# A decoder layer on one core: batch loops written out, attention without a gap between batches, buffers by parity in place of copies

## The chip, the cores and the metric

One core of a Trainium2 chip runs the whole program. The time is the device time of one execution in microseconds (us), median of several runs. Engines are named PE (matmul), PEld (its weight loads), DVE, ACT, POOL and SP; SP here only issues DMAs, and a DMA is waited for through a semaphore.

## The reference, cut to what matters

Eight batches of 512 positions with 256 features, float32. Three blocks, each added to its input:

```
x = x + mamba2_block(layernorm(x))         # in_proj, causal conv of 4 taps, silu, selective scan
x = x + attention(layernorm(x), ctx, ctx)  # 16 heads of 16; scores/4 + adj, masked keys at -inf
x = x + experts(layernorm(x))              # position picks 1 of 8 matrices 256x256 (+ bias)
```

Inside `mamba2_block` the input is normalised once more, then `z`, `xBC` (768 channels) and `dt` (8 heads) are projected, `xBC` goes through the convolution and silu, `dt` through softplus; the scan `h = h*exp(dt*A) + dt*x*B`, `y = h.C + D*x` runs over the 512 positions; `y*silu(z)` is RMS-normalised and projected back to 256. Attention takes its queries from the normalised result and keys and values from `ctx`, adds `adj` (512x512) and the mask to the scores, and projects with `Wo`. The experts are chosen by position alone, the same for all batches.

## The kernel before, in words

**Sizes.** 512 positions are C = 4 chunks of P = 128. The scan is done in chunks by matmuls: per chunk a decay matrix (`seg`, on `L`), the Gram matrix and transposes (`gx`), the gate projection (`z`), products with the carried state (`inter`), within the chunk (`intra`) and for the next state (`state`), then gate, RMS norm, transpose (`o`), output projection (`x1`) and the query's layer norm (`xq`).

**Attention units.** One unit is one head and one tile of 128 queries: UNITS = 64 in a batch, in G = 4 groups of UG = 16 units (four heads). For unit u, PE makes scores in `ps[u%2]` (`score`, the call through `mm`, L474), DVE adds the bias `am` and takes the row maximum into `T` and `nmx` (`take_max`, L1153), ACT takes the exponential in place (L806), and three units later (LAG) PE transposes the row block into `pt` (`turn`, L609), and ACT (L820) or, for five units of each sixteen, DVE (L1166) moves it to `PT`. After a group PE multiplies with the values (`pv`, L622, into `po`), ACT copies the sums to `OTs` (L824), PE turns them back (L629) and DVE divides (L1171, L1174). Q and K were written to DRAM in a high and a low part (`out_parts`) and are loaded two heads at a time into `q_st`, `k_st` (`stage`), eight DMAs each time; stage 0 of a batch is loaded before its attention, stage 1 at its start.

**Order of the work.** Every engine runs its own instruction list. The lists are built slot by slot from one table: slot u holds the attention's unit u of batch a and the stages of other batches that the tables `MAIN`, `CHUNK` (at slots 7, 17, 27, 37) and `NEXT` put there. One body has SLOTS = 64 + 15 slots. It works on three batches at a time: attention of a, everything from K to the queries of b = a+1, and the head (layer norms, `dt`, `bc` projections, convolution, `cum`) of a+2. In slots 64 to 78 no unit begins: the last units drain, the output projection runs over `ps` and `pt` (`project_turn` L636, `project`), and the rest of the next head is done. The bodies of the first two calls without attention, of a = 0 and of a = 6 and 7 are written out; those between are a hardware loop (`eng.Fori`), SP's with one batch fewer. Semaphore targets inside the loop are computed in registers (`alone`).

**Buffers.** Values, score bias and the residual rows are made in `vm`, `am_m`, `x1` and copied by DMA to `va`, `am`, `x1a` for the attention that follows. The smaller matmuls share three PSUM banks `pm` in a fixed rotation, `M_TILES`: 56 tiles a batch; a tile may be written when the tile three before it has been read (`m_full`, `m_read`).

**Beginning and end.** After the head of batch 0, `between` runs on all engines: a 1-of-8 routing of positions to experts, mostly on DVE with a few small matmuls. After the last attention come the experts: gather by position, layer norm, matmuls, scatter.

Of the kernel before, what the change touches and what calls it, by code (L numbers as in the profile page):

```python
# [42 lines left out]
PROJ = UNITS + LAG + 3  # L43

EVAC_DVE = (1, 5, 7, 11, 15)
DRAIN = 15
SLOTS = UNITS + DRAIN
NT = 8
PD = 32
# [15 lines left out]
HEAD = ("ln1", "ln2", "lnT", "dt1", "dt2", "bc", "conv", "cum")  # L65
# [3 lines left out]
MAIN = {  # L69
    ("k", 0): (0, {}), ("k", 1): (1, {}), ("ksplit",): (2, {"sp": 1}), ("v", 0): (2, {"dve": 1}), ("v", 1): (3, {"dve": 2, "sp": 1}),  # L70
    ("silu", 4): (1, {"dve": 1}), ("silu", 5): (2, {"dve": 1}), ("silu", 0): (3, {"dve": 2}), ("silu", 1): (4, {"dve": 1}),
    ("silu", 2): (5, {"dve": 1}), ("silu", 3): (6, {"dve": 1}), ("am", 0): (10, {}), ("am", 1): (12, {}), ("am", 2): (13, {}), ("am", 3): (16, {}),
    ("q1",): (50, {}), ("q2", 0): (51, {}), ("q2", 1): (52, {}), ("qsplit",): (53, {"sp": 1}),
}

CHUNK_AT = (7, 17, 27, 37)
CHUNK = {
    ("dmask",): (0, {}), ("seg", 0): (1, {}), ("seg", 1): (1, {}), ("gx",): (2, {"dve": 1, "pool": 1}), ("z",): (3, {"act": 1, "dve": 2}),
    ("w",): (4, {}), ("inter",): (5, {"dve": 1}), ("sdec",): (6, {}), ("intra",): (6, {"dve": 1}), ("state",): (7, {"dve": 2}), ("gate",): (8, {}),
    ("gate2",): (9, {}), ("o",): (9, {}), ("x1",): (10, {"dve": 1, "pool": 1}), ("xq",): (12, {}),  # L80
}

NEXT = {
# [4 lines left out]
}  # L88


def schedule():


    when = {e: [[] for _ in range(SLOTS)] for e in ("sp", "pe", "act", "dve", "pool")}

    def put(stage, slot, shift):
        for e in when:
            when[e][slot + shift.get(e, 0)].append(stage)
# [1317 lines left out]
```

## Time and profile before

| | |
|---|---|
| time, median of 3 runs (us) | 1533.87 (1533.64 to 1536.82) |
| span of the profiled execution (us) | 1529.4 |
| its own whole time | not listed beside the span; the median is 4.5 us above the span |
| instructions | 24283 |
| PE, DVE, ACT, POOL busy (us) | 1228.2, 1021.7, 776.9, 576.2 |
| mean granted PE clock | 0.932 of full speed |
| DMA | 117.20 MB, of which 1.62 MB instructions |

The span runs from the first to the last instruction of one execution. Busy time is the union of an engine's recorded instructions. Matmuls are pipelined and their ends are modelled, so PE's busy time is an upper figure. A time stands at the start of each row of a timeline; what is in square brackets behind a row is the engine's idle time before it and what ended it, "issue" meaning that nothing in the profile did.

### The profile page before, as it was taken

To read this page: it belongs to the slowest core of one execution; us is meant where nothing else is said; L and a number is where in the kernel's file an instruction comes from. 1 tells how busy PE (TensorE), PEld (TensorE's weight loads), DVE (VectorE), ACT (ScalarE), POOL (GpSimd) and SP (SyncE) were. 2 spreads that over 40 slices of the span, in tenths; PEclk is the share of its full clock that TensorE was granted. 3 is DMA by queue.
4 is the path that set the end of the run, shared out by engine and by line. 5 is a ranking of instruction groups with operands and counts; after the bars stand their busy time and mean duration, and the time that the engine had idled before them with its cause. 6 is when DMAs were issued, how large, how long until landed. Compare 5 with 4: busy or idle time off the path is not lost.

```text
span 1529.4 us, 24283 instructions
## 1 busy us (share of the span) xinstructions
PE 1228.2 (80%) x7020; PEld 787.0 (51%) x7020; DVE 1021.7 (67%) x2572; ACT 776.9 (51%) x1380; POOL 576.2 (38%) x533
## 2 busy tenths in 40 slices
PE   1577778878898789888888799878997889777488
PEld 1344445645565456555665456535654566454344
DVE  1655476876776577766687567758668667476376
ACT  0122156654566366645565356636564566577333
POOL 1725364335331723153333533172324532010165
PEclk9779789999999999988999899989999899999889
DMA  5020412134202331133212421234102321331321
GB/s 154 9 69 1 159 61 56 42 97 139 56 29 70 126 97 29 44 111 110 56 42 93 138 57 32 65 113 109 34 29 99 108 56 42 111 90 42 139 88 65
DMA packets 67713, 117.20 MB, mean 77 GB/s; under 512 B 16160, under 2 KB 26656, under 8 KB 65280
## 3 DMA queue, kind: packets, MB, share of 16 engines
q1 hardware_dynamic: 57808, 95.58, 19.5%
q0 software_dynamic: 6240, 17.57, 5.0%
q10 hardware_dynamic: 3536, 2.43, 0.6%
q8 instruction: 69, 1.13, 0.3%
q14 instruction: 60, 0.49, 0.1%
HBM read 71.49 MB, written 27.26 MB: 65 GB/s over the span
## 4 chain that ended last, share of the span: by engine, by line
PE 48%; DVE 25%; issue 13%; ACT 9%; POOL 3%; DMA 1%; SPq 1%; DVEq 1%; ACTq 0%; POOLq 0%
PE pm L474 21%; PE po L622 8%; DVE T L1153 6%; PE pt L609 5%; PE ps L474 4%; ACT PT L820 3%; ACT T L806 3%; PE ps L712 2%; PE pt L474 2%; DVE PT L1166 2%; DVE xc L1137 1%; DVE L L1061 1%; DVE xc L1142 1%; PE po L629 1%; DVE kp L1125 1%
## 5 line engine op out<-in xcount | busy, mean ns | idle before, releaser
L806 ACT ACTIVATE T<-T,nmx 128x512 f32<-128x512 f32 x512 | 369.2, 723 | 335.5 <-DVE nmx L1153 333.0
L1153 DVE CUSTOM_DVE_ANT_0 T<-ps,am 128x512 f32<-128x512 f32 x512 | 350.0, 687 | 272.3 <-PE ps L474 248.5
L609 PE MATMUL pt<-ident,T 128*128 128x128 f32 x2048 | 323.5, 283 | 63.2 <-ACT PT L820 62.6
L609 PEld LDWEIGHTS pt<-ident,T 128*128 128x128 f32 x2048 | 251.4, 145 | 175.3 <-ACT PT L820 59.6
L474 PE MATMUL ps<-k_st,q_st 128*128 128x512 f32 x512 | 306.6, 599 | 24.3 <-DVE nmx L1153 12.9
L820 ACT COPY PT<-pt 128x512 f32<-128x512 f32 x352 | 200.0, 571 | 55.1 <-PE po L622 54.4
L622 PE MATMUL po<-PT,va 128*32 128x512 f32 x1024 | 126.5, 638 | 29.7 <-DVE PT L1166 22.7
L474 PEld LDWEIGHTS ps<-k_st,q_st 128*128 128x128 f32 x512 | 101.9, 199 | 81.8 <-issue 59.2
L1244 POOL TENSOR_TENSOR xc<-xc,ygT 128x512 f32<-128x512 f32 x96 | 130.3, 1357 | 10.3
L1166 DVE COPY PT<-pt 128x512 f32<-128x512 f32 x160 | 109.8, 686 | 9.4 <-PE pt L609 9.0
L474 PE MATMUL pm<-xnT,wxbc 128*128 128x512 f32 x192 | 94.4, 625 | 0.0
L1295 POOL TENSOR_TENSOR rr<-se,nhalf 128x1 f32<-128x1 f32 x32 | 21.8, 681 | 191.8 <-DVE se L1096 191.8
L1273 POOL TENSOR_TENSOR xdt<-xt,dt 128x512 f32<-128x512 f32 x32 | 34.4, 1074 | 151.3 <-ACT xt L778 151.3
L474 PE MATMUL pm<-wout,ygT 128*128 128x256 f32 x256 | 66.8, 406 | 26.9 <-ACT ygT L786 26.7
L622 PEld LDWEIGHTS po<-PT,va 128*32 128x32 f32 x1024 | 32.6, 116 | 101.0 <-issue 73.4
L1241 POOL TENSOR_SCALAR ygT<-pre,cw 128x512 f32<-128x512 f32 x96 | 74.1, 772 | 9.8 <-POOL xc L1244 7.4
L474 PE MATMUL pm<-xdt,L 128*128 128x64 f32 x512 | 63.3, 277 | 12.1 <-issue 11.1
L474 PEld LDWEIGHTS pm<-xdt,L 128*128 128x128 f32 x512 | 60.2, 193 | 20.4 <-issue 20.4
L474 PEld LDWEIGHTS pm<-wout,ygT 128*128 128x128 f32 x256 | 47.9, 197 | 40.2 <-ACT ygT L786 21.2
L474 PE MATMUL pm<-L,stril 128*128 128x512 f32 x128 | 66.3, 644 | 0.8 <-POOL L L1265 0.8
L1265 POOL TENSOR_TENSOR L<-triu,dA 128x1024 f32<-128x1024 f32 x32 | 66.0, 2063 | 0.0
L1236 POOL TENSOR_SCALAR xc<-pre,cw,cb 128x512 f32<-128x512 f32 x32 | 28.6, 895 | 94.4 <-ACT pre L746 94.4
(208 smaller groups left out, 1995.3 us busy)
## 6 DMA issues: line engine op xcount, KB each, us to landing
qk_d<-kp SPq DMA_DIRECT2D x64, 256.0 KB, 2.4
q_st<-qk_d SPq DMA_DIRECT2D x256, 64.0 KB, 2.2
k_st<-qk_d SPq DMA_DIRECT2D x256, 64.0 KB, 2.2
am_m<-in_mask SPq DMA_DIRECT2D x8, 1024.0 KB, 7.4
am_m<-in_adj POOLq DMA_DIRECT2D x8, 1024.0 KB, 9.8
am<-am_m SPq DMA_DIRECT2D x16, 512.0 KB, 3.5
va<-vm SPq DMA_DIRECT2D x8, 1024.0 KB, 4.6
x_in<-in_x SPq DMA_DIRECT2D x8, 512.0 KB, 4.1
```

What stands on the lines that cost most here:

```text
L474: return pe.matmul(out, lhsT, rhs, start=first, stop=last)
L609: ins = pe.transpose(pt[u % 2][:, kt * P:(kt + 1) * P], T[:, u % RING, kt * P:(kt + 1) * P], ident[:, :])
L622: ins = pe.matmul(po[VW * hh:VW * (hh + 1), :], va[:, kt, g * HG + hh, :], PT[:, hh, kt, :], start=(kt == 0), stop=(kt == C - 1), tile_pos ...
L712: ins = pe.matmul(ps[w % 2][SEG * j:SEG * (j + 1), h * E:(h + 1) * E], t_f[:, w % 2, (h * KE + kt) * P + SEG * j:(h * KE + kt) * P + SEG * ...
L806: act.activation(T[:, u % RING, :], T[:, u % RING, :], ACT.Exp, bias=nmx[:, u % RING:u % RING + 1], scale=-1.0).then_inc(sems["probs"], 1)
L820: act.copy(PT[:, hh, :, qt * P:(qt + 1) * P], pt[v % 2][:, :].rearrange("p (k i) -> p k i", i=P)).then_inc(sems["evac_act"], 1)
L1153: dve.tensor_tensor_reduce(T[:, u % RING, :], ps[u % 2][:, :], am[:, qt, :], -1.0, 3e38, ALU.add, ALU.min, nmx[:, u % RING:u % RING + 1]). ...
L1166: dve.tensor_copy(PT[:, hh, :, qt * P:(qt + 1) * P], pt[v % 2][:, :].rearrange("p (k i) -> p k i", i=P)).then_inc(sems["evac_dve"], 1)
L1241: pool.tensor_scalar(tap[:, :, :].rearrange("p k i -> p (k i)"), src[:, j:j + S], cw[:, mt, j:j + 1], 0.0, ALU.mult, ALU.add).then_inc(sem ...
L1244: pool.tensor_tensor(xc[:, mt, :], xc[:, mt, :], tap[:, :, :].rearrange("p k i -> p (k i)"), ALU.add).then_inc(sems["conv_pool"], 1)
L1265: pool.tensor_tensor(dmask[:, :, :], triu[:, :].rearrange("p (o i) -> p o i", o=1).broadcast_to([P, NH, P]), dA[:, c, :].rearrange("p (h o ...
L1273: pool.tensor_tensor(xdt[:, :, :], xt[:, :, :], dt[:, c, :].rearrange("p (h o) -> p h o", o=1).broadcast_to([P, NH, HD]), ALU.mult).then_i ...
```

## The change: what it does

1. **Loops written out.** `batches`, `Fori`, `alone` and the register targets go. Each engine has one list over SLOTS = LEAD + 8 x 64 + 16 slots, LEAD = 92. `M_TILES` becomes a table of (tile, batch) over the whole program.
2. **No gap.** Unit u of batch a is at slot LEAD + 64 a + u; the next batch's unit 0 follows unit 63 directly, and the three units, the `pv`, and the projection that were in the drain now stand between the next batch's units.
3. **Stage table anew.** `STAGES`, `CHUNK`, `TAIL` give for each stage and each engine an own place, in slots (with fractions for the order within one) counted from the same batch's unit 0. `ln2` is split: `xn` at -82, `xr` (`ln2r`) at -65.75. The routing (`between`) is after slot -65 of batch 0.
4. **Buffers by parity.** `vas`, `ams`, `x1s` are pairs, used by batch parity; the copies `vm` to `va`, `am_m` to `am`, `x1` to `x1a` go. The mask for a batch is loaded two batches' buffers apart. A further memset prepares the second `va`. `xq` lies in `xr`, `xqT` in `th`.
5. **Output projection** as tiles `ot` (transposes) and `op` (matmuls) in the rotation of `pm`: 64 tiles a batch. It is at 69.5 to 77.5, in units 5 to 13 of the next attention.
6. **Waits** that the body's order gave are now written, mostly on tiles of batch b - 1; `more_consts` is waited for in single stages of batch 0.

```diff
-PROJ = UNITS + LAG + 3
-DRAIN = 15
-SLOTS = UNITS + DRAIN
+DVE_SETUP = 10
+SETUP_AT = -65
...
-MAIN = {
-    ("k", 0): (0, {}), ("k", 1): (1, {}), ("ksplit",): (2, {"sp": 1}), ("v", 0): (2, {"dve": 1}), ("v", 1): (3, {"dve": 2, "sp": 1}),
...
-    ("q1",): (50, {}), ("q2", 0): (51, {}), ("q2", 1): (52, {}), ("qsplit",): (53, {"sp": 1}),
+STAGES = {
+    ("ln1",): {"dve": -89.75, "pool": -89.5}, ("ln2",): {"dve": -82}, ("ln2r",): {"sp": -63.75, "dve": -65.75, "pool": -68},
+    ("lnT",): {"pe": -80.5, "act": -80.75}, ("dt1",): {"pe": -78.75, "act": -76.75, "dve": -78.5}, ("bc", 4): {"pe": -79, "act": -79.75},
+    ("conv", 4): {"pool": -71.75}, ("bc", 5): {"pe": -73.5, "act": -72.25}, ("conv", 5): {"dve": -70.25}, ("bc", 0): {"pe": -72, "act": -70.25},
+    ("conv", 0): {"pool": -70.25}, ("bc", 1): {"pe": -70.75, "act": -70.25}, ("conv", 1): {"dve": -66.5}, ("bc", 2): {"pe": -65.25, "act": -66},
+    ("conv", 2): {"pool": -59.5}, ("bc", 3): {"pe": -64.25, "act": -65}, ("conv", 3): {"pool": -55.5}, ("dt2", 0): {"dve": -76},
...
+    ("silu", 2): {"act": -59.5, "dve": -54.75}, ("silu", 3): {"act": -57, "dve": -54.75}, ("q1",): {"pe": -13.75, "act": -14},
+    ("q2", 0): {"pe": -12.75, "act": -11.5}, ("q2", 1): {"pe": -11.5, "act": -11.25}, ("qsplit",): {"sp": -9.5, "dve": -9.5}, ("first",): {"sp": -7.25},
 }
-CHUNK_AT = (7, 17, 27, 37)
+CHUNK_AT = (-56, -46, -36, -27)
 CHUNK = {
-    ("dmask",): (0, {}), ("seg", 0): (1, {}), ("seg", 1): (1, {}), ("gx",): (2, {"dve": 1, "pool": 1}), ("z",): (3, {"act": 1, "dve": 2}),
...
+    ("dmask",): {"pool": 1.5}, ("seg", 0): {"pe": 2.25, "act": 2}, ("seg", 1): {"pe": 1.5, "act": 1.5},
+    ("gx",): {"pe": 2.5, "act": 2.75, "dve": 3.25, "pool": 7.25}, ("z",): {"pe": 4.25, "act": 4.25, "dve": 5.25}, ("w",): {"dve": 5},
+    ("inter",): {"pe": 5.5, "dve": 6.5}, ("sdec",): {"pool": 8.75}, ("intra",): {"pe": 6.75, "dve": 7}, ("state",): {"pe": 7.5, "dve": 8.75},
+    ("gate",): {"act": 7, "dve": 7.25}, ("gate2",): {"dve": 8.25, "pool": 10.25}, ("o",): {"pe": 8.75, "act": 8.25},
+    ("x1",): {"pe": 10, "dve": 11, "pool": 11.75}, ("xq",): {"dve": 12.5, "pool": 19.25},
 }
-NEXT = {
-    ("ln1",): (47, {}), ("ln2",): (54, {}), ("lnT",): (55, {"sp": 1}), ("dt1",): (58, {"dve": 1, "act": 2}), ("bc", 4): (60, {}),
-    ("conv", 4): (61, {}), ("bc", 5): (62, {}), ("conv", 5): (64, {}), ("bc", 0): (64, {}), ("conv", 0): (65, {}), ("bc", 1): (65, {}),
-    ("conv", 1): (67, {}), ("bc", 2): (69, {}), ("conv", 2): (69, {}), ("bc", 3): (70, {}), ("conv", 3): (71, {}), ("dt2", 0): (60, {}),
+TAIL = {
+    ("ot", 0): {"pe": 70.25, "act": 69.5}, ("ot", 1): {"pe": 71.5, "act": 70.75}, ("ot", 2): {"pe": 71.75, "act": 71.5},
+    ("ot", 3): {"pe": 71.75, "act": 71.75}, ("op", 0): {"sp": 70.5, "pe": 71.75, "dve": 71.5}, ("op", 1): {"sp": 77, "pe": 72, "dve": 73.5},
+    ("op", 2): {"sp": 77, "pe": 77.25, "dve": 77.5}, ("op", 3): {"sp": 77.5, "pe": 77.25, "dve": 77.5},
 }
+LEAD = 92
+SLOTS = LEAD + B * UNITS + 16
...
-        x1, xq = sb("x1", [P, C, E]), xn
+        x1s = [sb(f"x1_{i}", [P, C, E]) for i in range(2)]
+        xq = xr
...
+        vas = [sb(f"va_{i}", [P, C, AH, VW]) for i in range(2)]
+        ams = [sb(f"am_{i}", [P, C, S]) for i in range(2)]
...
-        def batches(eng, body, peeled=0, between=None):
-            body(None, None, 0)
...
-            with eng.Fori(1, B - 2 - peeled) as a:
-                body(a + 1, a, a + 2)
...
+                    if k == "first":
+                        sp.wait_ge(sems["qk_out"], at("qk_out", b, 16 * 8))
+                        sp.wait_ge(sems["score"], at("score", b, -HS * C))
...
+                        stage(b, 0)
...
+                    if k == "ot":
+                        q = stg[1]
+                        pe.wait_ge(read(stg, b), free_at(stg, b))
+                        pe.wait_ge(sems["heads_normed"], at("heads_normed", b, G))
...
+                for s_ in range(SLOTS):
+                    a, u = divmod(s_ - LEAD, UNITS)
+                    if 0 <= a < B:
+                        score(a, u)
+                    a, v = divmod(s_ - LEAD - LAG, UNITS)
+                    if 0 <= a < B:
+                        turn(a, v)
...
+                    for stg, b in WHEN["pe"][s_]:
+                        m(stg, b)
+                    if s_ == LEAD + SETUP_AT:
+                        between()
...
+                    dve.memset(vas[1][:, :, :, :], 0.0).then_inc(setup["dve"], 1)
...
+                    if k == "op":
+                        q = stg[1]
+                        dve.wait_ge(full(stg, b), full_at(stg, b))
...
+                        dve.tensor_tensor(x1s[b % 2][:, q, :], bank(stg, b)[:, 0:E], x1s[b % 2][:, q, :], ALU.add).then_inc(read(stg, b), 1)
```

## Rows read from the trace of the kernel before

**Rows 1.** The page, part 1: span; an engine's busy us, share, instructions.

```profile
span 1529.4 us, 24283 instructions
...
PE 1228.2 (80%) x7020; PEld 787.0 (51%) x7020; DVE 1021.7 (67%) x2572; ACT 776.9 (51%) x1380; POOL 576.2 (38%) x533
```

**Rows 2.** The page, part 4: the chain that ended last, by engine.

```profile
PE 48%; DVE 25%; issue 13%; ACT 9%; POOL 3%; DMA 1%; SPq 1%; DVEq 1%; ACTq 0%; POOLq 0%
```

**Rows 3.** Busy time in stretches of the span; columns stand in the first line.

```profile
core 0: us, PE busy (x) PEld busy (x) DVE busy (x) ACT busy (x) POOL busy (x), PEclk, DMA share, GB/s
...
80.50:155.90 75.40, 57.17 (x209) 33.45 (x209) 41.11 (x90) 19.44 (x36) 31.77 (x29) 0.88 0.15 35
...
193.60:1192.40 998.80, 848.51 (x4580) 551.39 (x4581) 708.69 (x1765) 558.74 (x998) 393.14 (x368) 0.95 0.25 74
1192.40:1422.00 229.60, 189.16 (x1126) 124.48 (x1125) 156.24 (x413) 151.48 (x263) 46.47 (x44) 0.97 0.25 72
...
1325.90:1341.30 15.40, 11.46 (x78) 7.10 (x76) 3.83 (x13) 4.52 (x10) 1.80 (x2) 1.00 0.54 191
1341.30:1422.00 80.70, 62.10 (x414) 40.13 (x414) 56.29 (x162) 62.98 (x107) 4.39 (x5) 1.00 0.21 59
```

**Rows 4.** The same view: one period in parts, two gaps, the densest stretch.

```profile
580.00:620.00 40.00, 36.87 (x215) 24.65 (x214) 30.28 (x79) 25.78 (x47) 14.57 (x14) 1.00 0.13 34
...
1000.70:1030.70 30.00, 20.77 (x91) 10.35 (x90) 15.94 (x28) 6.52 (x14) 21.95 (x22) 0.88 0.35 125
1030.70:1167.80 137.10, 121.47 (x675) 81.56 (x674) 100.29 (x267) 86.41 (x152) 41.55 (x40) 0.96 0.22 62
1167.80:1192.40 24.60, 18.35 (x89) 9.59 (x88) 15.85 (x28) 6.52 (x14) 16.91 (x16) 0.93 0.33 118
...
1030.70:1192.40 161.70, 139.82 (x763) 91.14 (x762) 116.14 (x294) 92.92 (x166) 58.46 (x55) 0.96 0.24 71
```

**Rows 5.** Timeline of DVE and PE behind a jump and without one.

```profile
695.32 0.69 DVE L1153 CUSTOM_DVE_ANT_0 T<-ps,am 128x512 f32<-128x512 f32 x1 [5.02 <-issue]
...
1192.43 0.69 DVE L1153 CUSTOM_DVE_ANT_0 T<-ps,am 128x512 f32<-128x512 f32 x1
...
692.90 3.40 PE L474 MATMUL pm<-ctx_in,wk 128*128 128x512 f32 x4
...
1192.12 1.88 PE L474 MATMUL pm<-ctx_in,wk 128*128 128x512 f32 x4
```

**Rows 6.** Waits of PE from 1030.7 to 1192.4: total us, times, longest.

```profile
PE pt L609 <- ACT PT L820: 5.8, 9, 1.0
PE po L622 <- DVE PT L1166: 4.5, 1, 4.5
PE pm L474 <- ACT ygT L786: 3.3, 3, 1.4
PE pm L483 <- DVE xn L983: 2.8, 1, 2.8
```

**Rows 7.** Timeline of DVE: three taps of one convolution.

```profile
1170.36 3.92 DVE L1137 SCALAR_TENSOR_TENSOR xc<-pre,cw,xc 128x512 f32<-128x512 f32 x3
```

**Rows 8.** Groups by line, 1030.7 to 1192.4: busy, mean ns | idle before, releasers.

```profile
L1153 DVE CUSTOM_DVE_ANT_0 T<-ps,am 128x512 f32<-128x512 f32 x64 | 43.9, 687 | 38.5 <-PE ps L474 32.8 <-issue 5.3
```

**Rows 9.** Timeline of SP's queue and PE before the first attention.

```profile
166.83 1.79 SPq L378 DMA_DIRECT2D qk_d<-kp  x4
...
175.22 1.83 SPq L386 DMA_DIRECT2D k_st<-qk_d  x4
...
171.08 3.55 PE L474 MATMUL pm<-wdt,xnT 128*128 128x8 f32 x16 [0.96 <-ACT xnT L734]
```

**Rows 10.** The page, part 6: DMA issues, KB each, median us to landing.

```profile
k_st<-qk_d SPq DMA_DIRECT2D x256, 64.0 KB, 2.2
```

**Rows 11.** Timeline of PE: a matmul that waited for its pm bank.

```profile
196.47 1.19 PE L474 MATMUL pm<-ctx_in,wk 128*128 128x512 f32 x1 [4.68 <-ACT pre L746]
```

**Rows 12.** Groups by line over the span: a memset in set-up.

```profile
L951 DVE MEMSET vm<- 128x2048 f32 x1 | 1.8, 1765 | 0.5 <-DVE cb L949 0.5
```

More of the change, by code:

```diff
@@ L495, in m @@
                         for kt in range(KE):
-                            ins = mm(bank(stg)[:, :], wxbc[:, kt, stg[1] * P:(stg[1] + 1) * P], xnT[:, kt, :], kt == 0, kt == KE - 1)
-                        ins.then_inc(full(stg), 1)
+                            pe.wait_ge(read(("lnT", kt), b), read_at(("lnT", kt), b))
+                        pe.wait_ge(read(stg, b), free_at(stg, b))
+                        for kt in range(KE):
+                            ins = mm(bank(stg, b)[:, :], wxbc[:, kt, stg[1] * P:(stg[1] + 1) * P], xnT[:, kt, :], kt == 0, kt == KE - 1)
@@ L591, in score @@
+                    if k == "op":
+                        q = stg[1]
+                        pe.wait_ge(read(stg, b), free_at(stg, b))
+                        pe.wait_ge(read(("ot", q), b), read_at(("ot", q), b))
+                        for kt in range(KE):
+                            ins = mm(bank(stg, b)[:, 0:E], OnT[:, q % 2, kt, :], wo[:, kt, :], kt == 0, kt == KE - 1)
+                        ins.then_inc(full(stg, b), 1)
                 def score(a, u):
@@ L784, in m @@
                         c = stg[1]
-                        act.wait_ge(full(("yT", c)), full_at(("yT", c), b))
-                        act.copy(ygT[:, :, :].rearrange("p k i -> p (k i)"), bank(("yT", c))[:, :]).then_inc(read(("yT", c)), 1)
+                        if c:
+                            act.wait_ge(full(("out", c - 1), b), full_at(("out", c - 1), b))
+                        act.wait_ge(full(("yT", c), b), full_at(("yT", c), b))
+                        act.copy(ygT[:, :, :].rearrange("p k i -> p (k i)"), bank(("yT", c), b)[:, :]).then_inc(read(("yT", c), b), 1)
                     if k == "silu":
@@ L840, in between @@
                     act.wait_ge(setup["scaled"], 1 + KI)
[L842 removed]
+                for s_ in range(SLOTS):
+                    a, u = divmod(s_ - LEAD, UNITS)
+                    if 0 <= a < B:
+                        exp(a, u)
+                    a, v = divmod(s_ - LEAD - LAG, UNITS)
+                    if 0 <= a < B and evac_by(v) == "evac_act":
+                        evac(a, v)
+                    a, v = divmod(s_ - LEAD - PV, UNITS)
+                    if 0 <= a < B and v % UG == 0:
+                        take_sums(a, v // UG)
+                    for stg, b in WHEN["act"][s_]:
+                        m(stg, b)
+                    if s_ == LEAD + SETUP_AT:
+                        between()
                 def place(k):
@@ new lines, in _ @@
+                for s_ in range(SLOTS):
+                    a, u = divmod(s_ - LEAD, UNITS)
+                    if 0 <= a < B:
+                        take_max(a, u)
+                    a, v = divmod(s_ - LEAD - LAG, UNITS)
+                    if 0 <= a < B and evac_by(v) == "evac_dve":
+                        evac(a, v)
+                    a, v = divmod(s_ - LEAD - PV - 2, UNITS)
+                    if 0 <= a < B and v % UG == 0:
+                        norm_heads(a, v // UG)
+                    for stg, b in WHEN["dve"][s_]:
+                        m(stg, b)
+                    if s_ == LEAD + SETUP_AT:
+                        between()
```

699 lines of the change are left out of this document (336 added, 363 removed), and 1 row of the table NEXT.

## The prediction

> **What bounds the kernel now.** I read the page's busy shares first: over the span of 1529.4 us PE is busy 80% [rows 1], and nearly half of the chain that ended last is PE [rows 2]. Such averages hide stages, so I cut the span where an attention ends or begins (the first and last DVE row maximum of each batch) [rows 3]: 193.6 us before the first attention, 998.8 us in which six batches begin theirs, 229.6 us for the last two, and 1529.4 - 1422.0 = 107.4 us of expert layer. The six periods average 998.8 / 6 = 166.5 us. One period is an attention part of 64 units and a gap without any, in which the attention drains, is projected, and the next batch's head goes on. In the attention part PE is busy 121.5 of 137.1 us (89%), DVE 73%; in a gap of 30.0 us PE 20.8 and DVE 15.9 [rows 4]. So PE bounds the attention part, and in the gap nobody is full: PE, DVE and POOL (22 of 30) wait in turns.
>
> Next I compared gaps. The one at 1000.7 takes 30.0 us, the one at 1167.8 takes 24.6 with the same matmuls [rows 4]. The first ends in a jump back to the loop's start, the second runs on into written-out code. At a jump DVE stands 5.02 us with nothing to wait for; at the other place it goes straight on. The four matmuls behind the jump take 3.40 us, behind the straight run 1.88: after the stop PE ran at its lower clock level [rows 5].
>
> **Term 1, the loop's back edges.** PE, ACT, DVE and POOL loop over five batches, so there are four jumps: 4 x (30.0 - 24.6) = 21.6 us. Nothing covers them, as all engines jump together. The batches already written out (the first, and the one at 1192.4) show no stop of this kind, so I take straight-line code at nothing; its ends are 0 and +5 us in all.
> The Trainium skill (Advanced Engine Details and Errata, Control Flow Timing) gives about 108 ns for a compare and branch. By that figure the four jumps are an estimated 0.4 us, and if the rest of the stop had another cause that stays, the sum would be 21 us later. The same skill (Runtime: NRT & Kernel Launch, Instruction fetch mechanics) says that a taken branch outside the window already fetched must wait for its page, which would give the 21.6 us of the row.
>
> **Term 2, no gap.** A period without a jump is 161.7 us with 139.8 of PE [rows 4]. The change removes no PE work: the four projections (now `ot`, `op` in the pm ring) are the same matmuls. So the new period is 139.8 plus the idle that is left. Of the 21.9 us idle, rows 6 name these: 4.5 before `po`, because DVE has 3.9 us of convolution taps [rows 7] and the end of the time-step series queued ahead of an eviction. In the new table these convolutions are at -70.25 and -66.5, which is inside an attention (places 57 and 61 of the batch two before), so this wait of the last group goes. 3.3 before the `wout` matmuls, which wait for ygT: their slot is now one further behind the transpose of `o`; I take 2.5 off. 2.8 before lnT, where four xr operations no longer stand in DVE's queue at that place; I take 1.4 off. The 5.8 of PT waits are the attention's own chain and stay. 21.9 - 4.5 - 2.5 - 1.4 = 13.5. Two things come on top: each DVE convolution now holds back row maxima inside the attention, while PE has work queued that doesn't need them: two units at 62.1 / 64 = 0.97 us [rows 3] and one or two `bc` projections, of which four matmuls take 1.88 [rows 5]: 3.8 us. (Three taps are 3.92 us [rows 7], with the cheaper first one some 4.5.) 2 x 0.7 = 1.4. And 1 us goes, as PE's clock (0.93 in the gap, 0.96 in the period) no longer drops. 139.8 + 13.5 + 1.4 - 1 = 153.7.
> A second way: the densest stretch, the scan's chunks with attention beside them, has PE at 36.87 / 40 = 92% with DVE at 76% [rows 4]. The whole period at that density is 139.8 / 0.922 = 151.7, and DVE would be at 116 / 152 = 76%, just the mix that this stretch already runs at. Between the two I take 153. Six periods: 6 x 153 = 918, against 998.8: -80.8 us, which contains term 1.
> The last two batches: the gap of 15.4 us goes [rows 3]; its 11.5 us of PE go under the last attention, where PE idles 18.6 of 80.7 us. That attention is bound by the chain PE-DVE-ACT, so I let 4 us come back: -11.4.
>
> **Term 3, the start.** Now batch 1's head runs after batch 0's queries, and the first row maximum is at 193.6. In the new table the two are interleaved. The chain left is: query split done at 166.8 (SP issues its stores), loads of q and k issued until 177.05, landing 2.2 later [rows 9, 10] = 179.3. In front of q1, PE also gets batch 1's lnT, the 3.55 us of `wdt` [rows 9] and one `bc`: about 6 us, of which PE's idle in the chunks, 75.4 - 57.2 = 18.2 us [rows 3], hides some 4: +2. The second `va` needs a memset of 2048 columns in DVE's set-up, which PE waits for; one such is 1.8 us [rows 12]: +1.8. 193.6 - 183.1 = 10.5, taken as -11 (ends 0 and -20).
>
> **Edits taken at nothing.** The copies am, va and x1a by DMA go, one set of buffers per parity instead: they land beside other work today, and DMA is a quarter busy [rows 3]. With the cover gone, the last of them would cost what a load of q and k does, 2.2 us or more, once. The added waits (on tiles of the batch before) stand on events one or more slots old: 0, at worst on some of them the 5.8 / 9 = 0.6 us of an ordinary wait [rows 6]. The register-computed waits go; rows don't show them apart: between 0 and -3 per period, taken 0. The first loads for a batch (`first`, -7.25) take 12.5 us from split to landing against 9.5 slots x 2.4 = 23 us from the split: covered. Mask loads and their adj addition get a whole batch more of room. The expert layer's 107.4 us keep their chain (last projection, x2 store, gather): 0 +- 3.
>
> **Sum.** 1529.4 - 80.8 - 11.4 - 11 = 1426.2 us of span. The profiled execution's own whole time isn't listed beside its span; the median of the runs is 1533.87, 4.5 above it. I carry that over: 1430.7, say 1430.
>
> **Rivals.**
> *Only as dense as the average attention part.* PE 121.47 / 137.1 = 88.6%: the period is 139.8 / 0.886 = 157.8. For it: the last 18 slots of each batch now hold DVE's convolutions, layer norm and step series beside PE's twelve `bc` matmuls. Against: the chunk stretch is as heavy on DVE and reaches 92%. Six periods -52, end -8, start 0: 1469.4 + 4.5 = 1474.
> *Denser.* Everything PE waits for in rows 6 is placed later, only the PT waits remain: 96%, 145.6 per period. -125, -13, -18: 1373.4 + 4.5 = 1378. For it: PE's end times are modelled, so some recorded busy is latency that fills up; against: attention alone, free of all else, still leaves PE 23% idle.
> *It doesn't do what it says.* The next attention waits at its first unit (q, k loads, or the `v` tiles), and the gap only moves; then term 1 is all: 1529.4 - 21.6 + 4.5 = 1512. Against: the 23 us of cover above.
> *Slower: the pm ring.* The projection's eight tiles per batch move from ps and pt, idle in the gap, into the ring of three pm banks, 56 tiles before, 64 now. PE's queue is in order: a tile whose bank isn't yet read holds scores and transposes as well. Such a wait is seen once at length, 4.68 us [rows 11]. Seven batches with n such waits cost 7 x 4.68 n = 32.8 n; the gain of 103 us is used up from n = 3.1 of the eight; with four it is 1426.2 + 131 + 4.5 = 1562. Against: ACT and DVE read within a slot of the matmul in the table.
> *DVE is the bound.* Matmuls are pipelined, and part of PE's recorded busy may be latency that costs nothing once work stands ready; its weight loads are only 91.1 of 161.7 us, DVE's 116.1 is then the fullest [rows 4]. At 88.6% a period would take 131 us: 1426.2 - 6 x 22 + 4.5 = 1299. Against: in the densest stretch PE stands 3 us and DVE 10, and of DVE's 38.5 us of idle before the row maxima 32.8 are ended by a score of PE [rows 8]. The Trainium skill (Trainium Kernel Development and Optimization, Performance Expectations) speaks for this rival: it calls matmul busy a bad measure and LDWEIGHTS busy a good one.
>
> **How the numbers follow.** Forecast 44%, own range 1408 to 1452; average density 20%; denser 22%; gap only moved 8%; slower by the ring 4%; DVE-bound 2%. The time is the forecast's, 1430. Low 1372 takes in the denser case, high 1480 the average one; left out are the moved gap, the ring, DVE-bound and some edges. What can be told from no change is 0.2%, 3 us: faster 0.95, same 0.01, slower 0.04.
>
> **What would show it.** Right: row maxima of consecutive batches at one even distance, some 153 us apart, with no stretch over 6 us without one; no DVE wait of 5 us with "issue" behind it; PE 91% busy from the first to the last attention; first maximum near 183; the last 107 us unchanged. Wrong: PE below 89% there with `ps` or `pt` waiting for DVE taps (average density); PE waits on pm ended by ACT's OTs copy or DVE's x1 add (ring); a hole at each batch's first score ended by a DMA (moved gap); DVE over 85% (DVE-bound).

## The result, and the profile after

The kernel after takes 1373.5 us (median of 4 runs, 1370.8 to 1374.6) against 1535.3 us beside it: ratio 0.8946, 95% interval 0.8916 to 0.8976. That is 162 us less; the forecast was 1430, with a range from 1372 to 1480, so the measured time stands 1.5 us inside its lower end. One of experiment 9's six executions took 4051 us, for no cause that the record shows, and is left out of its ratio.

The page of the kernel after, part 1 (before: rows 1):

```profile
span 1372.8 us, 21799 instructions
...
PE 1166.6 (85%) x7020; PEld 768.3 (56%) x7020; DVE 993.5 (72%) x2574; ACT 774.3 (56%) x1380; POOL 579.1 (42%) x533
```

PE issues the same 7020 matmuls and is recorded busy 61.6 us less. So the change took away recorded busy time as well as waiting; the prediction had counted only 1 us a period for that.

Busy time by stretch, the kernel after: before the first attention, six periods, the last two batches, the expert layer, and one period alone (before: rows 3 and 4):

```profile
core 0: us, PE busy (x) PEld busy (x) DVE busy (x) ACT busy (x) POOL busy (x), PEclk, DMA share, GB/s
0.00:189.20 189.20, 114.05 (x382) 71.17 (x382) 100.65 (x215) 36.84 (x67) 83.41 (x81) 0.83 0.23 64
189.20:1046.30 857.10, 789.81 (x4510) 528.53 (x4511) 675.09 (x1755) 551.91 (x988) 389.88 (x361) 0.98 0.25 68
1046.30:1266.10 219.80, 189.85 (x1192) 128.18 (x1191) 155.69 (x421) 152.46 (x269) 52.80 (x51) 0.98 0.23 64
1266.10:1372.80 106.70, 72.88 (x940) 40.42 (x938) 62.09 (x187) 33.06 (x58) 53.00 (x42) 0.89 0.27 105
760.10:902.00 141.90, 131.47 (x767) 88.24 (x765) 113.11 (x297) 92.41 (x166) 64.95 (x61) 1.00 0.26 71
```

| part | before | after | change | forecast |
|---|---|---|---|---|
| start, to the first row maximum | 193.6 | 189.2 | -4.4 | -11 |
| six periods | 998.8 | 857.1 | -141.7 | -80.8 |
| last two batches | 229.6 | 219.8 | -9.8 | -11.4 |
| expert layer | 107.4 | 106.7 | -0.7 | 0 |
| span | 1529.4 | 1372.8 | -156.6 | -103.2 |

The surplus is nearly all in the six periods, 142.9 us each and not 153. Of their 141.7 us, 58.7 are PE's recorded busy time (848.5 to 789.8) and 83.0 its idle time (150.3 to 67.3). Of the 58.7, the clock column accounts for some 33 (0.05 x 998.8 less 0.02 x 857.1, as an estimate good to 9 us), and the 70 matmuls that moved ahead of the first attention for 13 at 0.18 us each; some 13 stay open. Set the last row beside the straight period of before [rows 4]: 161.7 us with 139.82 busy at clock 0.96, now 141.9 with 131.47 at 1.00, on four matmuls more. A clock column of 0.96 means that 8% of the time is at 1.2 GHz and not 2.4; if PE is busy in all of it, that is an estimated 0.04 x 161.7 = 6.5 us of the 8.3 us less busy.

The seam between two attentions, timeline of DVE, the kernel after (line 1166 is the row maximum):

```profile
759.53 0.69 DVE L1166 CUSTOM_DVE_ANT_0 T<-ps,am 128x512 f32<-128x512 f32 x1
...
760.14 0.69 DVE L1166 CUSTOM_DVE_ANT_0 T<-ps,am 128x512 f32<-128x512 f32 x1
```

The last row maximum of batch 3 and the first of batch 4, 0.6 us apart where 24.6 to 30.0 us stood. All six first maxima of the steady part follow their predecessors within 1.8 us.

Waits of PE in the six periods, the kernel after (us in total, times, longest):

```profile
PE pt L576 <- ACT PT L783: 25.0, 46, 0.8
PE pm L522 <- DVE yg L1090: 17.6, 18, 1.3
PE ps L421 <- DVE nmx L1166: 10.3, 9, 2.8
PE pm L421 <- POOL L L1281: 6.2, 4, 4.6
PE pm L421 <- issue: 5.7, 13, 0.9
```

And of the kernel before, 193.6 to 1192.4, the lines that went:

```profile
PE po L622 <- DVE PT L1166: 22.7, 5, 4.6
PE pm L474 <- ACT ygT L786: 20.1, 18, 1.5
PE pm L483 <- DVE xn L983: 16.6, 6, 2.8
PE ps L474 <- issue: 10.5, 4, 3.0
PE po L629 <- ACT OTs L824: 6.3, 12, 0.7
```

The waits of `po`, of `wout` for ygT and of lnT for xn are gone entirely; the wait for yg grew from 11.4 to 17.6. No wait for the ring's new tenants `ot` and `op` appears.

### The profile page after: what moved, and what is told of

It is laid out like the page before. It is cut to its first block, busy times and chain, and to the rows that moved or that the text cites. A ratio compares the mean times of both kernels' runs of the same rounds, so it can differ in the third digit from the quotient of the medians.

```text
span 1372.8 us, 21799 instructions
## 1 busy us (share of the span) xinstructions
PE 1166.6 (85%) x7020; PEld 768.3 (56%) x7020; DVE 993.5 (72%) x2574; ACT 774.3 (56%) x1380; POOL 579.1 (42%) x533
## 4 chain that ended last, share of the span: by engine, by line
PE 35%; DVE 20%; POOL 16%; issue 12%; ACT 7%; DMA 1%; DVEq 0%; POOLq 0%; ACTq 0%
PE pm L421 17%; POOL xc L1258 6%; DVE T L1166 5%; PE pt L576 5%; PE po L590 5%; POOL ygT L1255 4%; PE ps L421 3%; ACT PT L783 2%; ACT T L793 2%; PE ps L660 2%; DVE PT L1173 2%; POOL xc L1250 1%; DVE yg L1090 1%; ACT th L743 1%; POOL xdt L1289 1%
## 5 line engine op out<-in xcount | busy, mean ns | idle before, releaser
L576 PE MATMUL pt<-ident,T 128*128 128x128 f32 x2048 | 314.7, 277 | 49.8 <-ACT PT L783 47.0
L421 PE MATMUL ps<-k_st,q_st 128*128 128x512 f32 x512 | 299.7, 586 | 10.9 <-DVE nmx L1166 10.8
L421 PEld LDWEIGHTS ps<-k_st,q_st 128*128 128x128 f32 x512 | 98.5, 192 | 57.4 <-issue 36.1
L590 PE MATMUL po<-PT,va 128*32 128x512 f32 x1024 | 117.8, 601 | 0.8 <-ACT PT L783 0.8
L1317 POOL TENSOR_TENSOR rr<-se,nhalf 128x1 f32<-128x1 f32 x32 | 17.8, 557 | 226.4 <-DVE se L1096 226.4
L1255 POOL TENSOR_SCALAR ygT<-pre,cw 128x512 f32<-128x512 f32 x96 | 77.3, 805 | 6.3
L421 PEld LDWEIGHTS pm<-xdt,L 128*128 128x128 f32 x512 | 62.7, 200 | 24.3 <-issue 23.4
L1289 POOL TENSOR_TENSOR xdt<-xt,dt 128x512 f32<-128x512 f32 x32 | 37.9, 1186 | 67.8 <-ACT xt L738 66.5
L1281 POOL TENSOR_TENSOR L<-triu,dA 128x1024 f32<-128x1024 f32 x32 | 60.7, 1896 | 0.0
L421 PE MATMUL pm<-wz,xnT 128*128 128x512 f32 x128 | 60.4, 594 | 0.2
```

The lines of the kernel that those rows point to most:

```text
L421: return pe.matmul(out, lhsT, rhs, start=first, stop=last)
L576: ins = pe.transpose(pt[u % 2][:, kt * P:(kt + 1) * P], T[:, u % RING, kt * P:(kt + 1) * P], ident[:, :])
L590: ins = pe.matmul(po[VW * hh:VW * (hh + 1), :], vas[a % 2][:, kt, g * HG + hh, :], PT[:, hh, kt, :], start=(kt == 0), stop=(kt == C - 1), ...
L1255: pool.tensor_scalar(tap[:, :, :].rearrange("p k i -> p (k i)"), src[:, j:j + S], cw[:, mt, j:j + 1], 0.0, ALU.mult, ALU.add).then_inc(sem ...
L1281: pool.tensor_tensor(dmask[:, :, :], triu[:, :].rearrange("p (o i) -> p o i", o=1).broadcast_to([P, NH, P]), dA[:, c, :].rearrange("p (h o ...
L1289: pool.tensor_tensor(xdt[:, :, :], xt[:, :, :], dt[:, c, :].rearrange("p (h o) -> p h o", o=1).broadcast_to([P, NH, HD]), ALU.mult).then_i ...
```

## Experiments

All ratios are against the kernel before on the same chip. The kernel after wasn't run again beside them, and the kernel before had medians from 1532.4 to 1536.9 us on these chips, so a difference of 4 us or less from the 1373.5 of the kernel after tells nothing.

**1. The back edges alone.** The kernel before, with

```diff
-            with eng.Fori(1, B - 2 - peeled) as a:
-                body(a + 1, a, a + 2)
-            for a in range(B - 2 - peeled, B - 2):
+            for a in range(1, B - 2):
                 body(a + 1, a, a + 2)
```

> The kernel before, with its loop over batches 1 to 5 written out as straight code; slots, gap, copies and buffers stay. Theory (term 1): the four back edges cost 4 x 5.4 = 21.6 us, so 1535.3 - 21.6 = 1514 us, and no DVE wait of 5 us with nothing to wait for is left. Rival (a compare and branch of 108 ns, and the stop has a cause that stays in straight code): 1535 us. Third: straight code four times as long costs instruction fetch of its own: over 1514, toward or above 1535.

1517.8 us, ratio 0.990 (0.9869 to 0.9931): 15.4 us, interval 10.6 to 20.1. Its trace in windows, one attention part and the gap behind it:

```profile
532.10:671.50 139.40, 122.18 (x677) 82.32 (x676) 103.07 (x269) 86.74 (x152) 47.80 (x45) 0.95 0.25 71
671.50:696.20 24.70, 18.42 (x89) 9.90 (x88) 15.87 (x29) 6.52 (x14) 16.99 (x17) 0.93 0.33 117
```

The gaps take 24.6 to 24.7 us now, the first 25.4: the 5 us stops are gone, all four. But the attention parts of this trace take some 139.3 us where they took 136.2 to 138.9. So a jump cost all engines some 5 us in place and, by the medians, about 4 us net; the rival, that a branch costs next to nothing, is ruled out. What the engines did in the 5 us isn't shown. Why the attention parts got longer was not found either; the profiled execution is the longest of its four (1524.8 us), and its start alone took 5.9 us more than that of the kernel before (first row maximum at 199.5), so the traces show a smaller net gain, 10.4 us over the six periods.

**2. PE kept busy in the gap.** As experiment 1, and

```diff
+                            if u == PV + UG * (G - 1) and a < B - 2:
+                                pe.wait_ge(sems["row_max"], at("row_max", a, UNITS))
+                                for _ in range(4):
+                                    mm(ps[0][:, :], ident[:, :], wz[:, 0, :], True, True)
```

> As the written-out kernel, and in each gap but the last two PE multiplies four unused 128x512 tiles (about 3.4 us at the low clock, under 2 at the high one) while it waits for the last group's transposes; their result is read by nobody. Theory (PE pays for idle stretches twice: after one, its clock is at the lower level for some us): the clock stays up in more of the gap, so this kernel is 1 to 3 us per gap faster than the written-out one although it does more: 1496 to 1508 us, and PE's mean clock rises from 0.93 to 0.95 or more. Rival (the low clock in the gap lies beside waits and costs nothing): the same as the written-out kernel within 3 us, or slower by up to 6 x 1.9 = 11 us, as the tiles stand in PE's queue.

1508.4 us, ratio 0.9856 (0.9819 to 0.9893): 9.4 us less than experiment 1, though 48 matmul instructions more are executed. The intervals of the two ratios overlap, so the reading rests on the gaps in the traces. Timeline of PE ahead of the last `po`, first experiment 1:

```profile
675.70 0.60 PE L607 MATMUL pt<-ident,T 128*128 128x128 f32 x4
680.91 5.34 PE L620 MATMUL po<-PT,va 128*32 128x512 f32 x32 [4.61 <-issue]
```

then experiment 2:

```profile
664.26 3.60 PE L472 MATMUL ps<-wz,ident 128*128 128x512 f32 x8
669.02 3.64 PE L620 MATMUL po<-PT,va 128*32 128x512 f32 x32 [1.16 <-issue]
```

The same 32 matmuls take 5.34 us behind a stop of 4.61 us and 3.64 behind a filled one. A window over those 5.34 us, experiment 1, has the clock at 0.68, and (1 - 0.68) x 5.4 is the 1.7 us:

```profile
680.90:686.30 5.40, 5.34 (x32) 1.55 (x32) 4.21 (x4) 0.00 (x0) 2.73 (x3) 0.68 0.01 3
```

The gap shrinks from 24.7 to 23.0 us, each of the six alike (the first from 25.4), and its granted clock goes from 0.93 to 1.00:

```profile
659.60:682.60 23.00, 20.17 (x97) 10.87 (x96) 15.88 (x29) 6.51 (x14) 17.00 (x17) 1.00 0.35 126
```

So PE pays for a stop twice. The gain is at the small end of what the theory expected, and the mean clock rose to 0.931 to 0.938, not to the 0.95 that it asked for. Each unused tile is two instructions: the four take 3.60 us at the high clock, where the expectation had reckoned with under 2.

**3. The gap put back into the new kernel.** The kernel after with

```diff
+GAP = 15
+PERIOD = UNITS + GAP
-                    a, u = divmod(s_ - LEAD, UNITS)
-                    if 0 <= a < B:
+                    a, u = divmod(s_ - LEAD, PERIOD)
+                    if 0 <= a < B and u < UNITS:
```

and the like for each engine and for `schedule`.

> The kernel after, with the batches 79 slots apart in place of 64: 15 slots without attention units stand between two attentions again. Code written out, buffers in turn and every stage's slot counted from its own batch stay. Theory A (the overlap carries the gain): per period the gap's PE work of 20.8 us stands alone again, with less idle than the 24.6 us of before's straight gap: 12 to 16 us more than 142.9 us, 7 periods: 1373.5 + 84 to 112 = 1458 to 1486 us. Rival B (slots, buffers and written-out code carry most of it, and the gap was little): 3 to 6 us per period, 1395 to 1415 us. The rest up to the written-out kernel of before is then what slots and buffers bring.

1543.4 us, ratio 1.0065 (1.0043 to 1.0087), beyond both theories: slower than the kernel before. One confounding wait is plain in its PE waits (whole span):

```profile
PE ps L423 <- DMA k_st<-qk_d: 73.4, 14, 8.2
```

The first loads stand 7.25 slots ahead of the attention, and without units these slots are short. That called for the next run.

**4. The gap, with loads in time.** As experiment 3, and

```diff
+EARLY = 12
-    table = dict(TAIL) | dict(STAGES)
+    table = dict(TAIL) | {stage: {e: n - EARLY for e, n in where.items()} for stage, where in STAGES.items()}
```

with the chunks and the set-up 12 slots earlier as well.

> The kernel with 15 unit-free slots between attentions once more, with all stages of a batch's head, chunks and queries 12 slots earlier, so that the loads of q and k have attention slots in front of them, as in the kernel before, and not gap slots. Theory A (e4_gap15 was long mainly because PE stood 73 us for k_st in its gaps and 32 us for xn): these waits go, and a period is what the kernel before needs in straight code, 164 us, less the waits for ygT, xn and po (20 + 16 + 23 us over six periods in rows of before, 5 to 8 us a period): 156 to 159, so 1373.5 + 7 x 13 to 16 = 1465 to 1486 us. Rival B (the new slots fit only an attention beside them, and in a gap they wait whatever the loads do): a period stays near e4's 167.4 us, 1530 to 1545 us.

1542.2 us, ratio 1.0044 (1.0028 to 1.0061). The DMA waits are gone, the time is not: rival B. Its six periods, and PE's longest waits in them:

```profile
196.70:1200.50 1003.80, 851.37 (x4581) 568.32 (x4580) 702.65 (x1766) 562.95 (x995) 391.61 (x361) 0.94 0.22 59
```

```profile
PE pt L579 <- ACT PT L786: 33.7, 49, 1.3
PE ps L424 <- DVE nmx L1169: 32.2, 25, 1.9
PE pm L424 <- POOL L L1284: 24.3, 6, 4.0
PE pm L525 <- DVE yg L1093: 21.9, 18, 1.9
```

Written-out code, buffers in turn, no DMA copies and the new slots are all in this kernel, and together, with a gap, they are worth nothing against before. (A table made for a gap can do better: experiment 1, on the old slots, is 24 us faster than this one, and its six periods take 988.4 us; against these the kernel after wins 131 us, with slots and buffers in it.) Taking the gap out of this table is worth 1003.8 - 857.1 = 146.7 us over six periods, of which PE busy is 61.6 and idle 85.1. The granted clock tells why the same matmuls are busy longer: 0.94 is 12% of 1003.8 at the low level, 60 us lost at most; 0.98 is 4% of 857, 17 us lost; together an estimated 43 of the 61.6 us (the column's two digits leave 9 us either way). Seventy-one matmuls fewer within the window, 0.18 us each, are 13 more; some 6 stay open. The idle time shows as waits for the row maxima (32.2 against 10.3) and POOL's decay product L (24.3 against 6.2).

**5. A stop put into the new kernel.** The kernel after, and PE waits once per batch for two chained loads:

```diff
                         score(a, u)
+                        if u == 28:
+                            pe.wait_ge(pause, 16 * (2 * a + 2))
```

> The kernel after, with one stop of PE in the middle of each of the eight attentions: at unit 28 PE waits for two small chained loads, 2.2 us each and their issue, some 4.5 us. Theory A (a stop also costs the clock, as the gaps of before did): the cost of each is its length plus 2 to 5 us of slower matmuls behind it: 8 x 6.5 to 9.5 = +52 to +76 us, 1425 to 1450 us, and PE's time at the low clock grows by 40 to 80 us. Rival B (only the stop's length, or less since the chain PE-DVE-ACT has slack): +20 to +36 us, 1394 to 1410 us, and the clock hardly moves.

1409.6 us, ratio 0.9199 (0.9175 to 0.9222): 4.5 us a stop over the kernel after. The eight stops among PE's waits over the whole span, then the timeline of PE at one of them, then the page:

```profile
PE pt L583 <- DMA pad<-in_ident: 28.4, 8, 4.4
```

```profile
696.09 1.11 PE L583 MATMUL pt<-ident,T 128*128 128x128 f32 x4 [3.63 <-DMA pad<-in_ident]
697.00 3.62 PE L428 MATMUL pm<-wout,ygT 128*128 128x256 f32 x8
```

```profile
PE 1177.5 (83%) x7020; PEld 775.7 (55%) x7020; DVE 995.2 (70%) x2574; ACT 775.6 (55%) x1380; POOL 578.4 (41%) x533
```

A window over the 5 us behind the stop has the clock at 0.50:

```profile
696.00:701.00 5.00, 4.91 (x14) 3.99 (x15) 0.00 (x0) 0.58 (x1) 0.00 (x0) 0.50 0.01 3
```

In the kernel after the same eight `wout` matmuls, those of the second chunk, take 1.97 us, at full clock:

```profile
678.23 1.97 PE L421 MATMUL pm<-wout,ygT 128*128 128x256 f32 x8
```

The stops themselves are 28.4 us, PE's busy time grows by 10.9 (1177.5 - 1166.6), together 39 of the span's 41.8 us. The total is at the upper end of B's range, but a stop was 3.6 us long and not 4.5: the stops alone don't make it. The clock's part that theory A wanted is there, only smaller, 1.4 us a stop and not 2 to 5. This trace is of the longest execution of its five (1416.4 us); by the medians, 36.1 us apart, some 1.0 us a stop is left beside the 3.6.

**6. The old slots inside a chunk.**

```diff
-    ("gate",): {"act": 7, "dve": 7.25}, ("gate2",): {"dve": 8.25, "pool": 10.25}, ("o",): {"pe": 8.75, "act": 8.25},
-    ("x1",): {"pe": 10, "dve": 11, "pool": 11.75}, ("xq",): {"dve": 12.5, "pool": 19.25},
+    ("gate",): (8, {}), ("gate2",): (9, {}), ("o",): (9, {}), ("x1",): (10, {"dve": 1, "pool": 1}), ("xq",): (12, {}),
```

and the other entries of `CHUNK` in the same way.

> The kernel after with the slots inside a scan chunk as before (o at 9, x1 at 10, gate2 and inter earlier), chunks starting where they start after. Theory (the later slots of o and x1 took away PE's waits for ygT, 20.1 us in six periods before, and a part of those for yg): +15 to +25 us in the steady part, against it some 5 us given back at the start, where no attention fills the longer chunk: 1383 to 1395 us. Rival (in an overlapped schedule such waits are filled anyway, as the denser kernel has work queued): within 5 us of 1373.5, or faster by the start alone, 1368 us.

1404.0 us, ratio 0.914 (0.9118 to 0.9163), 30 us slower than after. PE's waits in its six periods, and those periods as a window:

```profile
PE pm L420 <- ACT ygT L748: 19.2, 18, 1.5
...
PE pm L521 <- DVE yg L1089: 6.6, 12, 0.6
```

```profile
184.40:1066.60 882.20, 802.61 (x4511) 532.25 (x4511) 681.99 (x1756) 551.97 (x986) 392.18 (x361) 0.98 0.24 66
```

The ygT wait is back at its old size and the periods are 4.2 us longer, 12.8 of the 25.1 us being busy time. The idle time grew by only 12.3 us, less than the 19.2 of ygT: all slots of the chunk moved, the wait for yg fell from 17.6 to 6.6, that for L (6.2) went, and that for PT rose from 25.0 to 32.2. So the run prices the chunk's slots together, not the wait for ygT. The first row maximum came at 184.4, 4.8 us earlier: without attention beside them the old slots are the shorter chain. The theory's direction held, its steady part at the very top of its range, and the start gave back what was expected; the last two batches took 5.9 us more on top, which it hadn't counted, and carried it beyond its range.

**7. The next wait, yg.**

```diff
-("o",): {"pe": 8.75, "act": 8.25},
-    ("x1",): {"pe": 10, "dve": 11, "pool": 11.75},
+("o",): {"pe": 9.75, "act": 8.25},
+    ("x1",): {"pe": 10.75, "dve": 11, "pool": 11.75},
```

> The kernel after, with PE's transposes of yg one slot later (9.75 for 8.75) and its wout matmuls three quarters of a slot later (10.75 for 10). Aimed at the second largest wait of PE, 17.6 us for yg in six periods. Theory (what PE waits for is what it loses, a later slot removes it, as it removed ygT's 20 us): up to 2.9 us a period, with the clock's part 1355 to 1365 us. Rival (a tile that waits longer in the ring of three banks, or a wout that now waits for ygT as before, takes the place of the wait): 1372 to 1390 us.

1388.5 us, ratio 0.9031 (0.9007 to 0.9054): 15 us slower. PE's waits in its six periods and their window:

```profile
PE pt L576 <- ACT PT L783: 39.2, 55, 1.1
PE pm L421 <- POOL L L1281: 15.2, 12, 4.6
...
PE pm L434 <- DVE xn L962: 5.9, 6, 1.0
```

```profile
193.40:1057.40 864.00, 786.23 (x4511) 528.71 (x4511) 672.94 (x1754) 552.05 (x986) 389.10 (x361) 0.99 0.25 68
```

No wait for yg is left, and still the idle time is 77.8 us against 67.3. It moved to PT (25.0 to 39.2), L (6.2 to 15.2) and xn, which are none of the places that the rival had named. Besides these 6.9 us of the six periods, the start took 4.2 us more and the rest 3.4. A wait's total is not what its removal brings.

**8. The copies.** The kernel after, and per batch, behind the first loads:

```diff
+                        for i, src in enumerate((va_b[:, 0:1024], va_b[:, 1024:2048], am_b[:, 0:1024], am_b[:, 1024:2048], x1_b[:, 0:1024])):
+                            sp.wait_ge(copied, 16 * (5 * b + i))
+                            sp.dma_start(copy_d[:, i * 1024:(i + 1) * 1024], src).then_inc(copied, 16)
```

> The kernel after, and per batch five copies of 0.5 MB by DMA (v tiles, masked bias, x1, to a scratch in DRAM), issued by SP behind the first loads of q and k; nobody reads the scratch. 21 MB more, about what the kernel before moved more (117.2 against 96.0 MB). Theory (edits taken at nothing): the copies lie beside other work, DMA is a quarter busy: 1373.5 within 3 us. Rival (their traffic and SP's waits, each behind the one before, delay the loads and stores of q, k and x2 that SP issues next): 2 to 6 us per batch, 1385 to 1420 us, with PE waits ended by k_st or q_st.

1375.4 us, ratio 0.8952 (0.8932 to 0.8973), against 0.8946 of the kernel after: nothing. Its six periods move 89 GB/s for 68 and take the same time:

```profile
189.70:1046.10 856.40, 789.88 (x4510) 529.07 (x4511) 674.75 (x1755) 552.15 (x988) 389.92 (x361) 0.98 0.31 89
```

The traffic costs nothing measurable here (these copies go to DRAM, those of the kernel before went from one on-chip buffer to another). That the buffers in turn were needed for the overlap is another matter; that wasn't tried.

**9. Batch 0 ahead.**

```diff
+AHEAD = 8
-for n, b, stage in sorted((where[e] + UNITS * b, b, stage)
+for n, b, stage in sorted((where[e] + UNITS * b - (AHEAD if b == 0 and stage[0] not in ("ot", "op") else 0), b, stage)
```

> The kernel after with all of batch 0's own stages 8 slots earlier than those of the other batches, counted from the attention (the other batches keep their slots). Batch 0's queries then stand ahead of batch 1's lnT, dt and bc on every engine, and these fill the 12.5 us in which q and k are split, stored and loaded. Theory (term 3 fell short by 6.5 us because batch 1's head stands ahead of batch 0's queries, q1 at 166.7 us against 155.9): the first row maximum comes 5 to 10 us earlier, 1364 to 1369 us. Rival (the scan's chain of batch 0 sets the start and batch 1's head was hidden; what moves behind the queries delays batch 1): same within 2 us, or up to 5 us slower as batch 1's head now runs late into attention 0.

1384.9 us, ratio 0.8999 (0.898 to 0.9018): 11 us slower, worse than the rival. Timeline of PE: the queries' transposes and the first scores, first the kernel after, then this one:

```profile
166.73 1.07 PE L536 MATMUL pm<-ident,xr 128*128 128x128 f32 x8
...
186.00 0.73 PE L421 MATMUL ps<-k_st,q_st 128*128 128x512 f32 x2
```

```profile
164.43 1.97 PE L537 MATMUL pm<-ident,xr 128*128 128x128 f32 x8 [2.58 <-DVE xr L1118]
...
193.89 1.02 PE L422 MATMUL ps<-k_st,q_st 128*128 128x512 f32 x2
```

The queries start only 2.3 us earlier, as they wait for the chunk's x1, and SP issues the first loads of q and k at the same time as before (180.5 us). Batch 1's head now begins later and still stands ahead of the first scores on PE, and ahead of the first row maximum on DVE, which comes at 199.9 us, 10.7 later. In this order, then, batch 1's head sets the start, not the round trip of the queries. In the kernel after it costs something too: DVE's `xr` and `xc` work of batch 1 stands between the scores, done at 186.7, and the row maximum at 189.2.

**10. Old slots for batch 0 alone.**

```diff
-for stage, where in table.items() if e in where)
+for stage, where in (table if b else first).items() if e in where)
```

where `first` has the old chunk slots of experiment 6.

> The kernel after, with the old slots inside a chunk for batch 0 alone; the other seven batches keep the new ones. Theory (the start fell short because batch 0's chunks have no attention beside them and the new slots stretch their chain; with old slots everywhere the first row maximum came at 184.4 us against 189.2): the start alone is won, 4 to 5 us, 1368 to 1370 us, and the periods stay at 142.9 us. Rival (batch 1's head, not the chunks, sets the first row maximum, as when batch 0 was put ahead): nothing, 1373 within 2 us.

1371.6 us, ratio 0.8937 (0.8911 to 0.8963). The first row maximum is at 185.7, 3.5 us earlier, somewhat less than the theory's 4 to 5, and the whole is within the error of the kernel after, and so inside the rival's range.

**11. The start filled.**

```diff
+                    if b == 0:
+                        for _ in range({"o": 2, "x1": 1, "q2": 1}.get(k, 0)):
+                            mm(ps[0][:, :], ident[:, :], wz[:, 0, :], True, True)
```

> The kernel after, and in batch 0 PE multiplies unused 128x512 tiles ahead of what it waits for: two ahead of each transpose of yg, one ahead of each wout and of each q2 projection, 14 in all (0.45 us each at the high clock, 0.9 at the low one); nobody reads them. Theory (the start's low clock, 65 of 189 us, is paid for because of such waits): the clock stays high from 110 us on, where 21 us were at the low level, and the first row maximum comes 3 to 8 us earlier, 1366 to 1370 us. Rival (the start is a chain of DVE, ACT and POOL, PE's speed is not in it): the 14 tiles lie in its waits, same within 2 us, or they stand in the way, up to 14 x 0.45 = 6 us slower.

1373.5 us, ratio 0.8936 (0.8913 to 0.8959): no change. The granted clock behind 156 us is up (0.86 over 155.9 to 189.2 in the kernel after),

```profile
156.00:189.00 33.00, 28.88 (x100) 15.15 (x98) 23.64 (x48) 11.51 (x21) 18.91 (x19) 1.00 0.21 64
```

and the first row maximum comes at 188.7 for 189.2. Over 110 to 156 us it rose only from 0.84 to 0.89, so the theory had its condition in part. The rival holds as far as the time goes: PE's speed is a small part of what sets the start. The 14 tiles are 28 instructions of 0.45 us, twice the work that the expectation had counted, and fit into PE's waits even so.

**12. Both.** The edits of 10 and 11 together.

> The kernel after, with batch 0's chunks on the old slots and with PE's 14 unused tiles ahead of its waits in batch 0. Apart, the first brought the first row maximum from 189.2 to 185.7 us, the second raised the granted clock behind 156 us from 0.86 to 1.00 and brought 0.5 us. Theory (the two add up, as the tighter chain now has PE in it more often): first row maximum at 182 to 185 us, 1366 to 1370 us. Rival (the tiles stand in the tighter chain's way): 186 to 189 us, 1371 to 1376 us.

1369.7 us (1368.9 to 1372.2), ratio 0.8939 (0.8917 to 0.896): the lowest median measured, but on the chip where the kernel before was fastest too (1532.4 us), and the ratio is no lower than those of experiments 10 and 11. The first row maximum was at 187.2, inside the rival's range, later than with the old slots alone: the two do not add up. That the time falls in the theory's range is no support for it.

## Why the forecast was right in kind and 57 us too long

- **No gap: right, and it carries the gain.** The attentions follow without a hole, PE is 92% busy in the six periods (forecast 91%). With the gap back in, the new kernel is no faster than before (3, 4). The slots inside a chunk have their part: with the old ones 25 of the 142 us of the six periods are lost again (6). Buffers in turn without the rest weren't tried. *Doesn't do what it says* is out: no score waits for a load at a seam.
- **Term 2, PE's busy time: the step that failed.** It said that the new period is "139.8 plus the idle that is left", less 1 us for the clock. Measured are 131.5. The prediction had seen in rows 5 that four matmuls take 3.40 us behind a stop and 1.88 without one, and used it for the jumps only; yet the stops of 3.2 to 4.6 us in experiments 1 and 5 do it too, and 0.96 in rows 4 already held 6.5 us a period. Experiments 2 and 5 show the mechanism from both sides. Its sum, 6 x 153.7 = 922.2 us, had 832.8 of busy time; it is 789.8. That is 43 of the 65 us between 922.2 and 857.1; idle time is the other 22. Of the 43, the clock accounts for an estimated 16 (6 x 6.5, less the 6 that were taken and the 17 that are still lost; 9 either way), and 68 matmuls fewer than six straight periods have (6 x 763 against 4510) for 12; some 15 stay without a cause shown. In the one period set beside the straight one it is 1.9 of 8.3. Recorded ends of matmuls are modelled, and stretches without a break may be recorded shorter; no run shows it.
- **Term 2, idle time: right in its items, too cautious.** Forecast 14.9 us a period, measured 67.3 / 6 = 11.2. `po` went as said (4.5), ygT whole (3.3, not 2.5), xn whole (2.8, not 1.4); PT fell from 5.8 to 25.0 / 6 = 4.2 where it was to stay. Added: yg, 1.0. That a named wait is worth its size is shown for neither: with ygT's wait the chunk's other waits moved too (6), and yg's only moved elsewhere (7).
- **Term 1: right in place, 6 us too large.** 15.4 us (10.6 to 20.1) and not 21.6. The Trainium skill (Advanced Engine Details and Errata, Control Flow Timing) gives 108 ns for a compare and branch; the measured price of about 4 us for a loop's end decides here. What the Trainium skill says elsewhere (Runtime: NRT & Kernel Launch, Instruction fetch mechanics), that a taken branch to code outside the pages at hand must first fetch it, would explain a stop, but it gives no time for it. That it "would give the 21.6 us" was more than the page says, and no run here tells such a fetch from another cost of the loop's end.
- **The last two batches: right** (-9.8 for -11.4), **the expert layer too** (-0.7 for 0).
- **Term 3: less than half.** -4.4 for -11. It charged batch 1's head with 2 us and the chunks with nothing. The new chunk slots stretch batch 0's chain by 3.5 to 4.8 us (6, 10), and batch 1's head stands before the first row maximum (9). Both together (12) did not add up, so the rest of the shortfall is open.
- **Edits at nothing: right.** The copies were measured (8). Of the *slower* rival, the pm ring, the trace of after shows six waits of 0.3 us at most, ended by DVE's addition of the scan's output to x1, 1.6 us in all; none is ended by a reader of `ot` or `op`.
- **The rivals.** *Denser* (145.6 us a period, 1378) is what happened, and beyond: 142.9. Its reason, that only the PT waits stay, was not quite it: idle was 11.2 and not 5.8 us, and the busy time fell instead. The range's lower end, 1372, had been drawn for this rival, so that 1373.5 lies inside it is partly luck. *DVE is the bound* did not come: DVE is busy 675.1 of 857.1 us, 79%, and PE's weight loads 62%. The rule of the Trainium skill that spoke for it (Trainium Kernel Development and Optimization, Performance Expectations: matmul busy is a bad measure) agrees in one respect: 59 us of matmul busy vanished in the six periods with the work the same but for 70 matmuls that moved before them, some 13 us at the mean of 0.18. But the largest part of that here is the clock, which the passage doesn't give as its reason.

## What to carry to other kernels

A PE busy time read from a kernel with stops is not a floor: look at the clock column, and take off (1 - clock) of the stretch before adding the idle that will be left. For the straight period that estimate is 139.8 - 6.5 = 133.3 us, and 131.5 were measured. It is of use only where PE bounds the stretch: at the start a clock of 1.00 in place of 0.86 brought 0.5 us (11). In this kernel a hole between two dense stages cost its idle time and, behind it, slower matmuls; overlap removed both. A wait that a trace names is a hint and no sum: moving PE's second largest away cost 15 us (7), and putting ygT's 19.2 us back added 12.3 us of idle time and 12.8 of busy time (6).

## What the runs showed of the hardware that was not expected

- A stop of PE of 3.6 us in a dense stretch costs 1.0 (by the medians) to 1.4 us (by the trace) of slower matmuls on average (experiment 5); 32 `po` matmuls take 5.34 us behind a 4.61 us stop and 3.64 without (2). Unused matmuls in the stop brought 1.7 us a gap back.
- The end of the loop that all engines close together costs about 4 us net and 5 in place (1); its cause is open.
- 21 MB more of DMA traffic, 89 for 68 GB/s over the six periods, cost nothing measurable (8).
